# Mixing the last group of batches on chip, and spreading the last but one group's iteration over more places

## The reference, cut to what matters

```
# stage 1: linear attention, per batch; q = layernorm(x), k = v = ctx
qh = softmax(Wq q over the 64 dims of a head) * SCALE;  kh = softmax(Wk k over the 2048 columns)
out = Wo ((kh vh^T) applied to qh) + bo;   x = x + out / |out| * g * 16
# stage 2: per row, seen as 4 streams of 512, xn = layernorm(x)
H_res = sinkhorn(W_res-logits / 0.1, 50 rounds)      # 4 x 4 per row
H_pre, H_post = softmax(...)                         # 4 per row
y = (sum_n xn_n * H_pre_n) @ W_branch                # 512 x 512
x_i = x_i + sum_j H'_ij xn_j + y * H_post_i
```

## Time and profile before

| | |
|---|---|
| median of 3 runs | 2567.82 us (2565.67 to 2569.39) |
| profiled execution: its time, its span | 2568.32 us, 2566.6 us |
| busy share PE, DVE, ACT, POOL | 94%, 67%, 46%, 43% |
| granted TensorE clock, mean of the span | 0.982 |
| DMA, mean | 100 GB/s |

### The profile page before, as it was taken

How to read it: one execution, slowest core, us unless ns; L and a number is a source line. 1 busy time by engine, 2 the same in 40 slices (tenths; PEclk the granted TensorE clock), 3 DMA queues, 4 the chain that set the end, 5 groups by cost and what they waited for, 6 DMA issues and landing times.

```text
span 2566.6 us, 35379 instructions
## 1 busy us (share of the span) xinstructions
PE 2413.9 (94%) x12004; PEld 1914.3 (75%) x12004; DVE 1726.8 (67%) x4114; ACT 1172.8 (46%) x2464; POOL 1094.4 (43%) x1107
## 2 busy tenths in 40 slices
PE   7999999999999999999999999999999999899774
PEld 6888878887878778787877778777778876777521
DVE  4454567676767557776776567667687756877786
ACT  4454444545354444545444454544445344453333
POOL 1635536172635427262543616245272633623410
PEclk9999999999999999999999999999999999999887
DMA  7112221313122432312213243343302233231376
GB/s 237 50 66 99 74 92 56 108 41 103 63 70 96 128 119 83 113 62 70 95 67 99 80 153 93 120 141 101 123 34 90 92 114 117 76 117 44 88 221 193
DMA packets 200145, 255.72 MB, mean 100 GB/s; under 512 B 43550, under 2 KB 109854, under 8 KB 199966
## 3 DMA queue, kind: packets, MB, share of 16 engines
q1 hardware_dynamic: 199966, 253.47, 31.3%
HBM read 177.53 MB, written 75.89 MB: 99 GB/s over the span
## 4 chain that ended last, share of the span: by engine, by line
PE 57%; DVE 20%; POOL 11%; issue 8%; ACT 3%; SPq 1%; DMA 1%; DVEq 0%; POOLq 0%; ACTq 0%
PE kc_bank L642 15%; PE big L701 7%; PE tb L743 4%; PE tb L757 3%; PE tb L628 3%; PE big L616 3%; PE big L618 3%; PE big L617 3%; POOL x_tr L1535 3%; DVE stats L889 3%; PE big L675 3%; PE big L677 2%; PE big L676 2%; PE tb L686 2%; POOL q_sb L1515 2%
## 5 line engine op out<-in xcount | busy, mean ns | idle before, releaser
L1254 ACT COPY turned<-tb 128x512 f32<-128x512 f32 x512 | 298.7, 587 | 755.3 <-PE tb L686 487.9
L701 PE MATMUL big<-merged,turned 128*128 128x256 f32 x2048 | 495.0, 385 | 36.3 <-ACT turned L1254 24.5
L642 PE MATMUL kc_bank<-ctxt,turned 128*128 128x256 f32 x2048 | 479.5, 380 | 3.0 <-DMA ctxt<-in_ctx_t 3.0
L701 PEld LDWEIGHTS big<-merged,turned 128*128 128x128 f32 x2048 | 385.8, 191 | 110.7 <-ACT turned L1254 19.4
L642 PEld LDWEIGHTS kc_bank<-ctxt,turned 128*128 128x128 f32 x2048 | 374.6, 191 | 54.6 <-issue 8.9
L1490 POOL TENSOR_TENSOR in_l<-x_sb,in_h 128x512 fp32r<-128x512 f32 x128 | 167.8, 1340 | 574.9 <-ACT in_h L1294 574.8
L1515 POOL TENSOR_TENSOR q_sb<-q_sb,qsum 128x1024 f32<-128x1024 f32 x128 | 243.8, 1904 | 274.4 <-DVE qsum L971 274.4
L980 DVE SCALAR_TENSOR_TENSOR on<-big,nrm,g_rows 128x256 f32<-128x256 f32 x256 | 111.9, 479 | 220.7 <-POOL nrm L1528 220.4
L616 PE MATMUL big<-in_h,wk_h 128*128 128x512 f32 x512 | 237.7, 464 | 15.4 <-DVE in_l L821 10.0
L675 PE MATMUL big<-wq_h,in_h 128*128 128x512 f32 x512 | 236.4, 462 | 10.9 <-DVE q_sb L959 10.4
L757 PE MATMUL tb<-mix_ld,mix_w 121*96 121x512 f32 (+2 forms) x324 | 187.9, 677 | 57.7 <-POOL mix_w L1497 28.0
(11 more groups left out here) (149 smaller groups left out, 4308.5 us busy)
## 6 DMA issues: line engine op xcount, KB each, us to landing
mix_ld<-streams SPq DMA_DIRECT2D x157, 240.0 KB
ctxt<-in_ctx_t SPq DMA_DIRECT2D x64, 512.0 KB, 4.0
x_sb<-in_x SPq DMA_DIRECT2D x64, 512.0 KB, 6.1
x_tr<-in_x_t SPq DMA_DIRECT2D x64, 512.0 KB, 6.6
streams<-x_sb SPq DMA_DIRECT2D x64, 512.0 KB, 3.1
stage<-in_ctx SPq DMA_DIRECT2D x60, 512.0 KB, 4.1
out<-mix_out SPq DMA_DIRECT2D x157, 192.0 KB, 2.2
streams<-y_sb SPq DMA_DIRECT2D x32, 256.0 KB, 2.0
```

The costliest lines, as they stand in the source:

```text
L642: t = nc.tensor.matmul(kc_bank[:, 0:C], turned[n % 3][:, j * P:(j + 1) * P], ctxt[:, nt, :], start=nt == 0, stop=nt == NT - 1)
L701: t = nc.tensor.matmul(big[2 + p % 2][:, half], turned[n % 3][:, dt * P:(dt + 1) * P], merged[:, dt, :], start=dt == 0, stop=dt == DT - 1)
L1254: nc.scalar.copy(turned[k % 3][:], tb[n % 2][:]).then_inc(s_tba, 1)
```

## The change

Four parts.

1. The list `free` of group 3 gets the places ("B", 14, 0, i), ("B", 15, 0, i) and ("B", b, 1, 0 and 1), and ends with ("Q", 15, 13) instead of ("Q", 15, 18). The same 116 calls are spread evenly over the new list. Calls by stretch, before and after: batch 14, key row 0: 0, 7; row 1: 4, 7; row 2: 14, 12; row 3: 13, 12; queries 5 to 9: 9, 9; 10 to 13: 8, 6; from 14: 11, 11. Batch 15: row 0: 0, 6; row 1: 4, 7; row 2: 14, 12; row 3: 13, 12; queries 5 to 9: 9, 9; 10 to 13: 8, 6; from 14: 9, 0.
2. No mix tile stands behind query places 14 and up of batch 15: three move to the tail, which has 53 in its iteration instead of 50. In these last queries PE runs `query_transpose` ahead of `attention_out`.
3. Batches 14 and 15 are no longer spilled, and their `y` and coefficients stay on chip: 8 spills of 512 KB, 4 stores of 256 KB and the stores of the coefficients go, and so do the last 11 mix tiles with their loads and DVE matrices.
4. The drain makes all 16 tiles of group 4 on chip: ten as before (ACT, then four additions on DVE, in five pairs), six on PE. For each of the six ACT scales the identity by five coefficients (L1350 of the kernel after), PE multiplies these five diagonal matrices with the five sources into one bank of `big` (L783), and ACT adds the bias (L1356).

```
-                 for n, size in enumerate((*GROUPS[:-1], GROUPS[-1] - 1))]
+                 for n, size in enumerate((*GROUPS[:-1], 0))]
...
+    OWN_PAIRS = 5
...
-        free = [place for place in order_of_places[starts[gr]:starts[gr + 1] - 8]
-                if place[0] == "Q" and 5 <= place[2] < NT + 4 or place[0] == "B" and (place[2] >= 2 or place[2:] > (1, 1))
+        free = [place for place in order_of_places[starts[gr]:starts[gr + 1] - (8 if gr < LAST - 1 else STEPS - 14)]
+                if place[0] == "Q" and 5 <= place[2] < NT + 4 or place[0] == "B" and (place[2] >= 2 or place[2:] > (1, 1) or gr == LAST - 1)
                 or place[0] == "A" and place[2] >= 2 and place[3]]
...
-        if place[0] != "Q" and place[2] == 0:
+        if place[0] != "Q" and place[2] == 0 or place[:2] == ("Q", NB - 1) and place[2] >= NT - 2:
...
+    for n in range(OWN - 2 * OWN_PAIRS):
+        if n < OWN_PAIRS:
+            put(TAIL, "own first", n)
+            put(TAIL, "own pair", n)
+        put(TAIL, "own diagonal", n)
+        if n >= 2:
+            put(TAIL, "own out", n - 2)
...
-                    if i >= 14 and (i - 14) % 4 == 0:
+                    if i >= 14 and (i - 14) % 4 == 0 and b < OWN_FIRST:
                         spill(b, (i - 14) // 4)
...
+                    elif task[0] == "own diagonal":
+                        n = task[1]
+                        w.wait_ge(s_diag, n + 1)
+                        if n >= 4:
+                            w.wait_ge(s_bias, n - 3)
+                        for j in range(PARTS):
+                            t = nc.tensor.matmul(big[n % 4], diagonal(n, j), own_source(2 * OWN_PAIRS + n, j), start=j == 0,
+                                                 stop=j == PARTS - 1)
+                        t.then_inc(s_prod, 1)
...
+                    first = b == NB - 1 and i >= NT
+                    if 4 <= i < NT + 4 and first:
+                        query_transpose(b, i - 4)
...
+            def own_diagonal(n):
+                w.wait_ge(s_skd, len(GROUPS) * SK_STEPS)
+                if n >= 2:
+                    w.wait_ge(s_prod, n - 1)
+                for j in range(PARTS):
+                    t = nc.scalar.activation(diagonal(n, j), ident[:], ACT.Identity, scale=own_coef(2 * OWN_PAIRS + n, j))
+                t.then_inc(s_diag, 1)
+
+            def own_out(n):
+                w.wait_ge(s_prod, n + 1)
+                k = 2 * OWN_PAIRS + n
+                nc.scalar.activation(own[k], big[n % 4], ACT.Identity, bias=own_bias(k)).then_inc(s_bias, 1)
```

More of the change, by code:

```diff
@@ L805, in tensor_program @@
                         return_pair(b, (i - 10) // 2)
-                    if 4 <= i < NT + 4:
+                    if 4 <= i < NT + 4 and not first:
                         query_transpose(b, i - 4)
@@ L1405, in behind @@
                             own_first(k)
+                    elif task[0] == "own diagonal":
+                        own_diagonal(task[1])
+                    elif task[0] == "own out":
+                        own_out(task[1])
                     elif task[0] == "center":
```

101 lines of the change are left out of this document (44 added, 57 removed).

## The result

The kernel after takes **2574.79 us** (median of 7 runs, 2573.02 to 2576.79), the kernel before 2567.82 (2565.51 to 2569.90, 7 runs). The ratio is **1.0026**, 95% interval 1.0017 to 1.0035: slower by some 7 us, where 2562.4 was forecast. The profiled execution took 2575.87 us; its span and busy shares stand on the page (columns: engine, busy us, share of the span, instructions).

What follows compares the result with a forecast made beforehand. PE was taken as the usual bound, waiting for DVE in places in the dense batches. Batches 14 and 15 -2.8, tail +0.8, drain -3.4 make -5.4 us, giving a median of 2562.4 us; range 2549 to 2577.

Steps and rivals of the forecast that it cites:

- Key rows 0 and 1: Batches 14 and 15: added calls delay ACT's exponentials, PE and a nearly full DVE; +10.3 us in 14, +9.2 in 15.
- Key rows 2 and 3: Batches 14 and 15: two calls fewer in row 2 save 2.1 us, one fewer in row 3 saves 0.7, per batch.
- The refresh: Key row 3 of batch 14: refresh moves from between ACT's exponentials to behind row 2's last; saves 3.5 of 4.1 us.
- Queries: Queries 10 to 13, batches 14 and 15: two calls fewer save 2.1 us of DVE each; 0 up to query 4.
- The last queries and the way into the tail: End of batch 15: nine calls go, leaving PE's own path from the last query maximum; saves 9.0 us, bounds 6 and 11.
- Tail and drain: Tail: added mix tiles cost +0.8 us, bounds 0 and 5. Drain: tiles on chip give -3.4, bounds -5 and -1.
- Rivals C and D: Drain: C, PE stays at 1.2 GHz, 2589 us, chance 0.05; D, PE starts each product low, 2572 us, chance 0.05.
- no series of groups behind waits: Drain of before: said against D that its trace shows no series of matmul groups each starting cold behind a wait.
- rival B: Key row 0: ACT's exponentials waiting for DVE's calls cost more than the queries give back; 2576 us, chance 0.17.
- My point from which B decides: B decides once rows 0 and 1 cost 5.4 us more than forecast, or the last queries give that much less.
- rival A: Key rows swallow the calls: lower bounds in rows 0 and 1, full prices elsewhere; 2554 us, chance 0.22.

Runs made afterwards that it cites:

- warm_half: Kernel after with unused matmuls (12, 10, 7, 7 and 4) put into PE's long waits in batches 14 and 15; 2569.0 us, ratio 1.0008.
- refresh_q: Kernel after with group 3's 49 later rounds cut into blocks of 17, 4, 5, 20, 3, putting every refresh into query places; 2570.0 us, ratio 1.0009.
- old_refresh_q: Kernel after with the `free` list of before and blocks of 14, 5, 5, 16, 9 rounds, putting all refreshes into query places; 2559.0 us, ratio 0.9968.
- warm_half_refresh_q: `refresh_q` with unused matmuls (12, 10, 7, 7 and 4) put into PE's long waits in batches 14 and 15; 2569.6 us, ratio 1.0004.
- old_list: Kernel after with the `free` list of before; drain on chip, tail and last queries without mix tiles stay; 2561.7 us, ratio 0.9975.

## Why the prediction was wrong, step by step

- *Key rows 0 and 1.* Right in mechanism and size: +10.9 and +10.2 for 10.3 and 9.2; the wait of PE 5.34 us for 5.5. Part of it (3.5 us in the two batches by `warm_half`, or 2.9 if its 0.6 is scatter) was PE's lower clock, which the working did not have; the calls themselves cost that much less.
- *Key rows 2 and 3: the step that failed.* It said that row 2 is DVE's, 2.1 us for two calls, and row 3 0.7 for one. Three calls fewer were worth -1.0 and +1.6 (24 against 27 calls, `refresh_q` against `old_refresh_q`), because they left places that PE's own 15.5 us cover. (Without the stalls behind POOL in row 3, 2.5 us by count, batch 15 would come to some -0.9 as well. That is an estimate; it is a third of the 2.8 forecast for three calls.) Even in before DVE waited 1.81 us for PE at the end of row 2 of batch 15: the row was not DVE's. The row I had argued from, busy DVE of a whole window, does not tell which calls are on the path; the chain does.
- *The refresh.* For row 3 of batch 14 I took 3.5 us; by `old_refresh_q` it is 2.3 there. The row did fall by 6.1, but row 2 grew by 2.7, since the refresh now stood behind PE's `y`; DVE waited 5.62 us for ACT's part of it there, and ACT for PE (the row below). And I looked only at the refresh that left: in batch 15 another one came into row 3 from the queries. Such a move was in the numbers of the list, and I priced one side of it. It cost 1.4 us there, and the third one 2.0 in row 1 (by `refresh_q`).

```profile
2136.67 0.19 DVE L1097 TENSOR_TENSOR sku<-sku,skr 128x32 f32<-128x32 f32 x1 [5.62 <-ACT skr L1368]
```

- *POOL.* That a multiplication of DVE waits for POOL's operation to end, and beside the subtraction lasts up to four times as long, was in no term, though the trace of before has such rows. In row 3 of batch 15 it is up to 4.2 us.
- *Queries.* -3.1 and -2.7 for -2.1 each, and +1.0 and +2.0 in the stretch to query 4, which I had at nothing. The last queries and the way into the tail gave 8.6 for 9.0.
- *Tail and drain.* +1.8 for +0.8, within its bounds and within the scatter of the tail, and -3.5 for -3.4. That this last number is so near is luck in part: the forecast ended the drain with six stores behind the last pair (33.3, landed at 34.6), and what ended it was the last bias at 32.0 and its own store, 2.5 us. Rivals C and D did not come: the granted clock was 0.68 around the first PE tile and 1.00 from 2549.6 on, with products behind each other. The working also said that the drain of before has no series of groups behind waits; it has one more, at 2556.42 behind a wait of 4.40 us, and it too started at the lower level (3.69 us for two tiles).

Rows 2 and 3 with the queries to the 4th were forecast at -9.1 us and measured at +2.4: that is 11.5 of the 12.9 us between the forecast (-5.4 on the span) and the result (+7.5). The time came out where rival B had it (2576), but not by its way: rows 0 and 1 cost 1.6 us more than I had said in all, not 5.4, and the last queries gave what I had said. My point from which B decides was therefore wrong too. What I had as rival A, that key rows swallow calls, is true of rows 2 and 3, and for that reason little could be gained by taking calls away from them.

What stays open: row 3 of batch 15 takes 2.8 us more in the kernels with the new list and the refreshes out than in `old_refresh_q`. Four DVE multiplications of 0.87 to 1.35 us in the one (`warm_half_refresh_q`) against two of 0.54 and 0.57 in the other make 2.5 of it, by count; that was not tried by itself. Calls were not taken out of B places alone, with all else left: that they return nothing is read from the length of PE's stretch and from DVE's wait. And how much of the 3.2 us by which the iteration of the tail grew in `old_list` is the added mix tiles is not known: with 50 tiles it took 103.3 and 103.6 us, with 53 between 103.8 and 106.8.

## What to carry to other kernels

Before work is moved between places of an in-order program, price each place on the chain and not by an engine's busy share: a place beside another engine's uninterrupted stretch is free until it is full, and what is taken from it returns little or nothing. List for every periodic step (here the refresh) where it stood and where it stands now, in all batches, since an even spread moves all of them. And where one edit makes the matmul engine wait, add the slower clock behind the wait to the bill.
